# A running maximum over all edges in place of segment maxima in one edge pass of a graph network kernel

## The reference, cut to what matters

```python
def _L0_gnn_ref(h, adj, direction, W_forward, W_reverse, attn_forward):
    h_fwd = h @ W_forward.T
    h_rev = h @ W_reverse.T
    src, dst = (adj[0], adj[1])
    messages = h_fwd[src] * direction[:, 0:1] + h_rev[src] * direction[:, 1:2]
    scores = jnp.einsum('ef,hf->eh', messages, attn_forward[0])
    scores = jax.nn.leaky_relu(scores, negative_slope=0.2)
    exp_scores = jnp.exp(scores - scores.max(axis=0, keepdims=True))
    sum_exp = jax.ops.segment_sum(exp_scores, dst, num_segments=N)
    norm = exp_scores / (sum_exp[dst] + 1e-10)
    outs = [jax.ops.segment_sum(messages * norm[:, hd:hd + 1], dst, num_segments=N) for hd in range(H)]
    out = jnp.stack(outs, axis=1)
    return out.reshape(N, -1)
```

## Time and profile before

| what | value |
|---|---|
| device time, median of 3 runs | 8171.8 us (8169.69 to 8186.81) |
| span of the profiled execution | 8112.0 us |
| median less that span | 59.8 us |
| PE, DVE, ACT, POOL busy in the whole span | 5601.5, 4057.9, 2838.0, 3138.4 us |
| the stage of the change | 1113 to 1880 us, 767 us |
| PE, DVE, ACT, POOL busy in it | 513.53, 480.80, 515.32, 416.44 us |

### The profile page before, as it was taken

How to read it: one execution, slowest core, us unless ns; L and a number is a source line. 1 busy time by engine, 2 the same in 40 slices (tenths; PEclk the granted TensorE clock), 3 DMA queues, 4 the chain that set the end, 5 groups by cost and what they waited for, 6 DMA issues and landing times. The chain is left out here.

```text
span 8112.0 us, 86982 instructions
## 1 busy us (share of the span) xinstructions
PE 5601.5 (69%) x21290; PEld 3555.5 (44%) x21290; DVE 4057.9 (50%) x9795; ACT 2838.0 (35%) x7825; POOL 3138.4 (39%) x3209
## 2 busy tenths in 40 slices
PE   2222547677699778887785568698857866888576
PEld 1111325445355356653343345354545543555343
DVE  5325836665311389994434333423456675555501
ACT  4223627664122144430102333122246633555110
POOL 3663035553466166640005662100056634555011
PEclk9999965557799878778997778799956666787588
DMA  2221521111010255540002221100033423333122
GB/s 84 69 65 42 173 66 43 40 39 16 26 32 20 74 157 159 160 129 14 8 27 87 84 85 39 38 33 30 14 103 106 110 66 92 89 91 90 54 109 69
DMA packets 272398, 573.85 MB, mean 71 GB/s; under 512 B 87398, under 2 KB 138138, under 8 KB 265242
## 3 DMA queue, kind: packets, MB, share of 16 engines
q0 software_dynamic: 134496, 314.63, 15.5%
q1 hardware_dynamic: 137530, 254.96, 9.6%
HBM read 520.14 MB, written 49.19 MB: 70 GB/s over the span
## 5 line engine op out<-in xcount | busy, mean ns | idle before, releaser
L1288 POOL DMA_INDIRECT L_edges_rows<-scratch_L_kv,L_edges_index x416 | 491.1, 1180 | 392.5 <-PE L_edges_ps_sum L1533 221.5
L1288 POOL DMA_INDIRECT L3a_edges_rows<-scratch_L3a,L3a_edges_index x416 | 442.6, 1064 | 472.7 <-DMA L3a_edges_last<-order_dst_last 256.7
L1288 POOL DMA_INDIRECT L3b_edges_rows<-scratch_L3b,L3b_edges_index x416 | 396.8, 954 | 460.1 <-PE L3b_edges_ps_sum L1533 296.7
L1288 POOL DMA_INDIRECT L_edges_rows<-scratch_L,L_edges_index x416 | 416.4, 1001 | 372.2 <-DVE L_edges_msg L1335 199.2
L1730 POOL TENSOR_TENSOR L_norm_fold<-L_norm_square 128x400 f32<-128x400 f32 x64 | 66.5, 1040 | 1262.2 <-ACT L_norm_square L1739 1262.2
L676 POOL DMA_INDIRECT L_edges_rows<-scratch_L,L_edges_index x416 | 396.8, 954 | 394.2 <-SPq L660 145.6
L499 POOL DMA_INDIRECT scratch_by_dst<-dst_record,dst_dest x400 | 406.2, 1016 | 315.0 <-DVE dst_dest L338 195.6
L518 POOL DMA_INDIRECT scratch_by_src<-src_record,src_dest x400 | 387.7, 969 | 266.9 <-issue 110.1
L688 PE MATMUL L_edges_ps_sum<-L_edges_rows,L_edges_hot 128*128 128x256 f32 x832 | 271.1, 466 | 222.7 <-issue 122.8
L400 PE MATMUL rank_ps_count<-rank_parts,rank_ident_b 128*128 128x225 bf16 x200 | 53.6, 370 | 534.6 <-DVE rank_parts L312 423.9
L2376 DVE TENSOR_TENSOR L_experts_gated_h<-L_experts_hidden,L_experts_share_rows 128x800 f32<-128x800 f32 x112 | 111.0, 992 | 609.5 <-ACT L_experts_hidden L2366 535.0
(11 more groups left out here) (761 smaller groups left out, 13494.6 us busy)
## 6 DMA issues: line engine op xcount, KB each, us to landing
x<-scratch_dst_key_rows SPq DMA_DIRECT2D x50, 512.0 KB
x<-scratch_src_key_rows SPq DMA_DIRECT2D x50, 512.0 KB
L_experts_w<-in_L_w SPq DMA_DIRECT2D x16, 1024.0 KB
L_edges_rows<-scratch_L,L_edges_index POOLq DMA_INDIRECT x832
L_edges_lo_rows<-order_src_lo_rows SPq DMA_DIRECT2D x52, 256.0 KB
L3a_edges_lo_rows<-order_dst_lo_rows SPq DMA_DIRECT2D x52, 256.0 KB
L3b_edges_lo_rows<-order_dst_lo_rows SPq DMA_DIRECT2D x52, 256.0 KB
x<-scratch_dst_lo_rows SPq DMA_DIRECT2D x50, 256.0 KB
```

The lines of the kernel that those rows point to most:

```text
L1288: pool.indirect_dma_start(rows[:, n % RING, k, 0:RW], None, row_table, bass.IndirectOffsetOnAxis(index[:, t:t + 1].bitcast(U32), 0)).then_ ...
```

## The change

For kind "dual" the maxima of the segments are no longer found. The tile scans, the chain scans, the two copies and the widening scans go, and with them the walls that SP fetched. In their place stands one number per head, the largest score of all batches so far, in `highest`, with two turns of which the older is kept. `tile_maxima` becomes one reduce of the transposed scores over 128 elements on 32 partitions; `row_maxima` one matmul that turns the 32 maxima into a row; `chain_maxima` a reduce of that row over the 8 tiles of each head, a maximum with the older value, and the fall as the older less the newer; `column_maxima` one matmul of a row of ones with `highest`, which spreads the four numbers to all 128 partitions and so takes the place of `turn_back` too. `widen` and `turn_back` return at once. `lower` subtracts and lists the four numbers with a broadcast over the eight tiles, where it had 32 columns. The factor of the fall works on `acc` as before. The other kinds are unchanged. The order of steps on each engine stays. DVE's waits for PE go from four to three: `turned`, `rowed`, `returned`.

```diff
--- before.py
+++ after.py
@@ -1193,6 +1193,7 @@
         ends = s.sb("ends", [1, 2, P])
         column = s.sb("column", [R, 2])
         fall = s.sb("fall", [1, H])
+        highest = s.sb("highest", [1, 2, H])
         factor = s.sb("factor", [1, H])
         minus = s.sb("minus", [1, 1])
         if kind == "dual":
@@ -1267,6 +1268,8 @@
                             sp.wait_ge(columns_hot, n - 1)
                         sp.dma_start(lo_rows[:, b, :], order["lo_rows"][n * SB:(n + 1) * SB, :]
                                      .rearrange("t p -> (t p)").partition_broadcast(P)).then_inc(lined[b], 16)
+                    if kind == "dual":
+                        continue
                     if n >= 2:
                         sp.wait_ge(widened, n - 1)
                     for h in range(H):
@@ -1341,6 +1344,10 @@
 
                 def tile_maxima(n, c, wall_turn):
                     b = c % 2
+                    if kind == "dual":
+                        dve.wait_ge(turned, n + 1)
+                        v.tensor_reduce(tops[0:R, 0:1], ps_a[0:R, 0:P], X, ALU.max).then_inc(maxed, 1)
+                        return
                     dve.wait_ge(walled[b], wall_turn * (16 * (H + 1)) + 16 * (H + 1))
                     dve.wait_ge(turned, n + 1)
                     link(v.tensor_tensor_scan(runs[:], wall[:, b, 0:P], ps_a[0:R, 0:P], -BIG, ALU.add, ALU.max))
@@ -1351,6 +1358,14 @@
                     b = c % 2
                     L = H * SEQ
                     dve.wait_ge(rowed, n + 1)
+                    if kind == "dual":
+                        old, new = highest[:, 1 - b, :], highest[:, b, :]
+                        link(v.tensor_reduce(new, ps_a[0:1, ROW:ROW + R].rearrange("o (h k) -> o h k", h=H), X, ALU.max))
+                        link(v.tensor_tensor(new, new, old, ALU.max))
+                        if c >= 1:
+                            dve.wait_ge(fell, n)
+                        v.tensor_tensor(fall[:], old, new, ALU.subtract).then_inc(chained, 3)
+                        return
                     link(v.tensor_tensor_scan(chain_run[:], chain_wall[:, b, 0:L], ps_a[0:1, ROW:ROW + L], -BIG, ALU.add,
                                               ALU.max))
                     link(v.tensor_tensor_scan(chain_top[:, ::-1], chain_wall[:, b, L:0:-1], chain_run[:, ::-1], -BIG,
@@ -1377,6 +1394,12 @@
                     dve.wait_ge(returned, n + 1)
                     if c >= 1:
                         dve.wait_ge(weighted, n)
+                    if kind == "dual":
+                        v.tensor_tensor(shifted[:].rearrange("p (h k) -> p h k", h=H), score.rearrange("p (h k) -> p h k", h=H),
+                                        bcast(ps_a[:, BACK:BACK + H], SB, 2), ALU.subtract).then_inc(lowered, 1)
+                        v.tensor_tensor(values(c)[:, :, F:M], bcast(ps_a[:, BACK:BACK + H], SB, 1),
+                                        bcast(last[:, ds(n * SB, SB)], H, 2), ALU.mult).then_inc(listed, 1)
+                        return
                     v.tensor_tensor(shifted[:], score, ps_a[:, BACK:BACK + R], ALU.subtract).then_inc(lowered, 1)
                     v.tensor_tensor(values(c)[:, :, F:M], by_head(ps_a[:, BACK:BACK + R]), bcast(last[:, ds(n * SB, SB)], H, 2),
                                     ALU.mult).then_inc(listed, 1)
@@ -1448,6 +1471,7 @@
                     link(v.memset(x[:], 0.0))
                 link(v.memset(chain_wall[:, :, H * SEQ:H * SEQ + 1], -BIG))
                 link(v.memset(minus[:], -1.0))
+                link(v.memset(highest[:], -BIG))
                 v.memset(acc[:], 0.0).then_inc(merged, BANKS)
                 dve.wait_ge(loaded, 64 if kind == "dual" else 48)
                 dve.wait_ge(merged, BANKS)
@@ -1491,6 +1515,10 @@
                     row = ps_a[0:1, ROW:ROW + H * SEQ].rearrange("o (h q) -> o h q", h=H)
                     ident = kit.ident[:, 0:R].rearrange("r (h k) -> r h k", h=H)
                     pe.wait_ge(maxed, n + 1)
+                    if kind == "dual":
+                        nc.tensor.matmul(ps_a[0:1, ROW:ROW + R], tops[:, 0:1], kit.ident[:, 0:R], start=True,
+                                         stop=True).then_inc(rowed, 1)
+                        return
                     nc.tensor.matmul(row[:, :, 1:SEQ:2], tops[:, 0:1], ident, start=True, stop=True)
                     nc.tensor.matmul(row[:, :, 2:SEQ:2], tops[:, P - 1:P], ident, start=True, stop=True)
                     nc.tensor.matmul(row[:, :, 0], kit.ones[0:1, 0:1],
@@ -1499,12 +1527,18 @@
 
                 def column_maxima(n, c):
                     pe.wait_ge(chained, n * 3 + 3)
+                    if kind == "dual":
+                        nc.tensor.matmul(ps_a[:, BACK:BACK + H], kit.ones[0:1, :], highest[:, c % 2, :], start=True,
+                                         stop=True).then_inc(returned, 1)
+                        return
                     for j in range(2):
                         ins = nc.tensor.matmul(ps_a[:, COL + j:COL + j + 1], ends[:, j, :], kit.ones[0:1, 0:1],
                                                start=True, stop=True)
                     ins.then_inc(columned, 1)
 
                 def turn_back(n, c):
+                    if kind == "dual":
+                        return
                     pe.wait_ge(widened, n + 1)
                     nc.tensor.transpose(ps_a[:, BACK:BACK + P], tops2[:], kit.ident[:]).then_inc(returned, 1)
```

## The result

The changed kernel takes 8139.3 us (median of 5 runs, 8124.9 to 8150.7) where the kernel before takes 8184.6 (5 runs, 8169.7 to 8204.0). The ratio is 0.9942, with a 95% interval of 0.9924 to 0.9960, so it saves some 45 us. The forecast was 8117 us within 8035 to 8165. The sign holds, and so does the size by the timed runs. Of the steps behind the size some don't, and two of the misses work against each other.

What follows compares the result with a forecast made beforehand. DVE's queue was taken to bound short batches, POOL's gather runs to stretch long ones. Short 25 + long 42 - added long batches 14 + start 2 = 55 us; 8171.8 - 55 = 8117 us, range 8035 to 8165.

Steps and rivals of the forecast that it cites:

- DVE's sum: First layer's edge pass, DVE's queue: about 1.9 us less work per batch, short batches 11.4 to 9.5 us if nothing else came.
- What is late next: Short batches: POOL's gathers at 10.5 us become the limit, so 28 batches save 0.9 us each, 25 us.
- The long batches: Batches tied to the end of a gather run: work removed behind the last long wait saves 42 us over 20 batches.
- the start: First batches of the stage, tied to POOL's run of 48 gathers: 2 us saved.
- the 14 us: POOL's pause between gather runs shrinks to 0.3 us, making 24 long batches instead of 20: 4 x 3.5 us lost.
- The first (hand-overs alone): Rival: DVE's hand-overs to PE, not POOL, carry the long waits; 84 us and 2 at the start, 8086 us; chance 0.14.
- The second (the long waits mostly go): Rival: fewer hand-overs meet a run of gathers, so long waits mostly vanish; 160 us saved, 8012 us; chance 0.13.
- The third: Rival: nothing comes of it, pairs of batches being paced by two gather runs; about 11 us, 8161 us; chance 0.12.
- The fourth: Rival: slower, POOL running 32 gathers unbroken at 29.5 us each time; three such give 8205 us; chance 0.08.
- The page against the row: Rule that engine and DMA ports can't contend, set against rows showing PE, ACT and DVE held during gathers; no size given.
- The 59.8 us: Gap between the profiled span of 8112.0 us and the median of 8171.8, taken as untouched by the change.

Runs made afterwards that it cites:

- the pair of one session: Kernel before and changed kernel, unedited, profiled a second time in one session: 8175.7 us (ratio 0.9998) and 8144.5 us (0.9952).
- fillers: Changed kernel plus four DVE scans per batch, right behind the hand-over of the scores or at the step's end: 8101.9 us (0.9893) or 8107.8 us (0.9905).
- the filler ahead: Changed kernel plus four DVE scans per batch, right behind the hand-over of the scores to PE: 8101.9 us, ratio 0.9893.
- the paced kernel before: Kernel before with POOL's gathers in this stage released one by one by merges, on a chip without holds: 7294.2 us, ratio 1.0005.
- the paced form of the changed one: Changed kernel with POOL's gathers in this stage released one by one by merges: 8056.5 us, ratio 0.9839.

## Why the prediction was right, and where it was not

*DVE's sum held.* I put it at 1.9 us a batch, from 11.4 to 9.5. The shortest batches after are 9.5 us. The new reduce L1349 takes 277 ns (0.28 forecast), L1363 and L1364 175 and 157 ns (0.15 each), the broadcast forms cost nothing (L1398 178 ns, 186 before). DVE's busy time fell by 4057.9 - 3958.5 = 99 us, with 100 forecast.

*What is late next was half right.* I let POOL's 10.5 us bound the short batches, so 25 us. With holds, they came to 10.0, and 26 of them saved 37 us. The step that failed is that POOL must keep up within a short batch: there are four row buffers, and it catches up in the long batch that follows. Without gathers the mean is 9.99 too, which is ACT's 10.04 us. Without holds POOL is the bound at 10.26 us a batch, as forecast.

*The long batches were the miss.* I had them save 42 us, less 14 for a stricter turn. They saved nothing: 22 of 18.85 and 19.17 us in place of 20 of 17.84 and 19.07, and not 14 to 17 us long. In the pair of one session the stage's 27 us are 6.1 at the start, 26 x (11.46 - 9.98) = 38.5 in the short batches, 2 x (19.17 - 11.46) = 15.4 lost in two that turned long, and 2 lost in the other twenty. The step that failed is the 14 us. I saw that the pause between two runs shrinks and counted a few more long batches, at 3.5 us each; but DVE's short batch of 9.6 us is now shorter than POOL's run of eight (10.1 to 10.3), so the pause goes altogether, and DVE meets each run of sixteen at its first hand-over with 9 us of it still to come. What that costs used up the 42 us too. By the difference between the changed kernel's stages and those with fillers it is 47 to 59 us, although the latter have 1.8 us more work in each batch; in that, the hand-over that one filler covers is not kept apart from the pause. With the filler ahead, where the short batches are 11.47 us and the runs are of eight as before, the long ones are 15.08 us, 20 x (17.84 - 15.08) = 55 to 20 x (19.07 - 15.08) = 80 us less than before. So long batches could be shortened; whether what I counted for the 42 us would have done it alone, no run shows.

*The rivals.* The first (hand-overs alone) fell with the kernels without gathers. The second (the long waits mostly go) fell with the trace: 22 long batches of 48 are left, and the waits at hand-overs grew from 135 to 205 us. The third came near in a pair of traces: the two profiled executions at hand when the result came differ by 6.5 us in the stage, since one was quick; the timed runs decide against it. The fourth named the mechanism: POOL, owing more than one batch, runs unbroken. It comes at sixteen gathers in every second batch and not at thirty-two a few times, and it took more than half of the 72.5 us that the change is worth without gathers. I had given it 8 in 100, as a case that takes all.

*The page against the row.* By the Trainium skill (SBUF — State Buffer, "SBUF: two separate sides") engine ports and DMA ports can't contend. The run with SP's DMAs agrees: 56 GB/s in its window and 12.9 us of waiting at the first hand-over in 40 batches. I had set the rule up against a hold by POOL, and named the second rival where the first was meant. That was a wrong use of it: the rule speaks of ports, and no run here shows that a port is what holds DVE and ACT. It remains that ACT, which shares no port with POOL by that page, is held as well (L1630 and L1634 above).

*A wrong term that did no harm.* The 59.8 us between the median and the profiled span are not work outside the span. In every run listed since, the device time is 1.7 to 1.8 us above its own span (8138.9 and 8137.1 for after). The profiled execution was simply 58 us quicker than the timed ones. It was quicker in stages with gathers: against the second execution 26.5 us in this edge pass, 10.8 in the third layer's sum pass and 14.9 in the first edge pass of the fourth layer (659.5 us against 674.4).

*The size.* Forecast 55, measured 39 and 45 us by the timed runs, 27 by the stages of one session. The stage of one and the same kernel differs by 26 us between two executions, so what lies between 27 and 45 isn't resolved by these traces. That 55 comes so near is in part luck: the stage was forecast at 690 us and took 744 and 750, the short batches and the start gave more than I had counted (45 us in place of 27), the long ones took 17 where I had counted on 28 of gain.

## What to carry to other kernels

Where two engines take turns at being late, making the quicker one quicker can let the other's bursts grow together; read the pause between its bursts, and ask whether it survives. An engine that is held up by another's burst is to be costed by where in its step the burst catches it, not by its busy time. A change to POOL's waits, which spreads the gathers, was worth twice the change itself here, so try the pace of a producer before taking work out of its consumer.

## What the runs showed of the hardware

While POOL issues indirect gathers, ACT and DVE can be held. DVE stood idle up to 11 us for a matmul that had long ended, and ACT 3.87 us for an operation of its own; PE took up what DVE handed over within 0.31 us. The holds lie in the later part of a burst: in a run of sixteen at DVE's hand-over 11 us in and not at the one 2 us in, and in two runs of eight with 0.85 us between them in the second. The same bytes moved by SP's plain DMAs (56 GB/s) hold nobody. And this depends on the chip: on two chips the kernel before takes 8184 and 8188 us, on two others 7284 and 7295 us, and on one of these POOL issues 416 gathers in one unbroken run with 1.0 us of waiting at the first hand-over in 46 batches. The gathers aren't slower where there are holds: those of the third layer's sum pass have a median of 953 ns on both kinds. Of the 900 us more than 300 lie ahead of this stage, which starts (L1335) at 1124.3 us in the second execution of before and at 795.9 in the paced kernel before: in the sort, where POOL scatters, DVE's last L253 begins at 781.1 and at 377.5 us. I haven't looked at what DVE waits for there. The third layer's sum pass takes 655.3 us with holds and 522.8 without, on the same code:

```profile
L676 POOL DMA_INDIRECT L_edges_rows<-scratch_L,L_edges_index x416: 949/953/1177, 3676.9 to 4199.7; - x139
```

What differs between these chips, and which part of a gather it is that holds the others, stays open. The gain of the change is the same on both kinds within the intervals (0.9942 and 0.9952 against 0.9947), though for different reasons: with holds it is 1.4 us in half of the batches, without them 11.4 us of DVE become 10.26 of POOL in all of them. Of the kernels that give the reference's output, the paced form of the changed one is the fastest measured where there are holds (0.9839); where there are none, pacing cost the kernel before nothing (1.0005), and the paced changed kernel was not run.
